# First attention of a two-layer kernel: row-paired score matmuls, and terms spread one batch earlier

## The reference, cut to what matters

```python
q = x @ Wq.T + bq ; k = x @ Wk.T + bk ; v = x @ Wv.T + bv     # 16 heads of 8
q = apply_rope(q) * scale ; k = apply_rope(k)
dots = einsum('bnih,bnjh->bnij', q, k)                        # 256 x 256 per head
dots = where(i < j, -100000.0, dots)                          # causal
attn = softmax(dots, axis=-1)
o = einsum('bnij,bnjh->bnih', attn, v)
out = o @ Wo.T + bo
```

## Time and profile before

| what | value |
|---|---|
| median of 3 runs | 1365.34 us (1360.61 to 1385.27) |
| the profiled execution | 1355.89 us |
| its span | 1354.0 us, 25150 instructions |
| first attention | from about 15 us to 444 us of the span |
| busy, TensorE / VectorE / ScalarE / POOL | 82% / 60% / 36% / 22% |
| mean granted TensorE clock | 0.88 of full speed |

### The profile page before, as it was taken

One profiled execution on the slowest core, in us unless ns is written; L12 is line 12 of the kernel. 1 busy time (PEld: TensorE's weight loads), 2 busy tenths in 40 slices (PEclk: granted clock), 3 DMA queues, 4 the chain that ended last, 5 costly groups with the idle time before them and its releaser, 6 DMA issues. The chain is left out here.

```text
span 1354.0 us, 25150 instructions
## 1 busy us (share of the span) xinstructions
PE 1105.7 (82%) x9345; PEld 654.5 (48%) x9345; DVE 815.0 (60%) x1910; ACT 483.5 (36%) x839; POOL 298.3 (22%) x283
## 2 busy tenths in 40 slices
PE   3699999999999599999999996588888889845140
PEld 2235454544444244444444442376777667744130
DVE  4456666646552466566666653488888888646322
ACT  0024444424445133323323321455555564411020
POOL 4132323213210000000000002342332321015536
PEclk9969999959999699999999998589999999855575
DMA  4534242422420622321332230323223322040233
GB/s 128 143 97 96 51 95 49 94 48 49 96 51 3 230 80 94 104 90 63 124 96 95 62 126 0 111 80 97 78 68 96 96 65 81 1 125 26 71 105 85
DMA packets 83989, 113.38 MB, mean 84 GB/s; under 512 B 9658, under 2 KB 53616, under 8 KB 81664
## 3 DMA queue, kind: packets, MB, share of 16 engines
q1 hardware_dynamic: 81840, 108.65, 28.5%
q0 software_dynamic: 2048, 3.37, 0.9%
HBM read 80.18 MB, written 32.65 MB: 83 GB/s over the span
## 5 line engine op out<-in xcount | busy, mean ns | idle before, releaser
L672 DVE TENSOR_REDUCE a_nmax<-ps 128x2 f32<-128x512 f32 (+1 forms) x192 | 132.4, 691 | 127.7 <-PE ps L513 88.2
L437 ACT ACTIVATE a_pr<-ps 128x512 f32<-128x512 f32 x192 | 114.2, 597 | 173.9 <-PE ps L488 124.9
L861 ACT ACTIVATE e_sg<-ps 128x512 f32<-128x512 f32 x136 | 81.2, 597 | 244.6 <-PE ps L886 231.5
L1050 DVE TENSOR_TENSOR e_up<-e_sg,ps 128x512 f32<-128x512 f32 x128 | 88.0, 687 | 106.9 <-PE ps L893 100.9
L886 PE MATMUL ps<-e_hT,e_wg 128*128 128x512 f32 x272 | 140.8, 600 | 0.8 <-DVE e_wT L1037 0.8
L902 PE MATMUL ps<-e_hm,e_wd 128*128 128x512 f32 x272 | 139.2, 594 | 1.4 <-DVE e_hm L1053 0.7
L472 PE MATMUL ps<-a_mask,identb 128*128 128x256 bf16 (+1 forms) x384 | 129.1, 336 | 13.5 <-DMA a_ks<-a_terms_d 9.4
L893 PE MATMUL ps<-e_hT,e_wu 128*128 128x512 f32 x272 | 139.8, 596 | 0.0
L1053 DVE TENSOR_TENSOR e_hm<-e_up,e_wb 128x512 f32<-128x512 f32 x128 | 88.5, 692 | 5.6
L902 PEld LDWEIGHTS ps<-e_hm,e_wd 128*128 128x128 f32 x272 | 51.5, 190 | 67.3 <-issue 63.5
L893 PEld LDWEIGHTS ps<-e_hT,e_wu 128*128 128x128 f32 x272 | 52.1, 191 | 65.6 <-issue 59.8
(11 more groups left out here) (266 smaller groups left out, 2031.6 us busy)
## 6 DMA issues: line engine op xcount, KB each, us to landing
e_wb<-e_wT_d SPq DMA_DIRECT2D x128, 256.0 KB, 3.3
a_gw<-a_gd_d SPq DMA_DIRECT2D x16, 1024.0 KB, 5.0
a_gd_d<-a_gc SPq DMA_DIRECT2D x64, 132.0 KB, 2.3
a_terms_d<-a_parts SPq DMA_DIRECT2D x32, 192.0 KB, 2.1
a_qs<-a_terms_d SPq DMA_DIRECT2D x16, 384.0 KB, 5.0
a_ks<-a_terms_d SPq DMA_DIRECT2D x16, 384.0 KB, 6.0
a_terms_d<-a_parts SPq DMA_DIRECT2D x32, 128.0 KB, 2.1
a_terms_d<-a_parts SPq DMA_DIRECT2D x32, 64.0 KB, 1.8
```

The costliest lines, as they stand in the source:

```text
L437: nc.scalar.activation(dst, src, ACT.Exp).then_inc(exp_done, 1)
L672: nc.vector.tensor_reduce(dst, src, AX_X, ALU.max, negate=True).then_inc(m_read, 1)
L861: nc.scalar.activation(sg[:, par], ps[:, 2 + par], ACT.Silu).then_inc(silu_done, 1)
L1050: nc.vector.tensor_tensor(up[:, par], sg[:, par], ps[:, 4 + par], ALU.mult).then_inc(up_done, 1)
```

## The change

In words:

1. **Pairs.** The terms of q and k are kept twice in `qs` and `ks`: in partitions 0 to 47 for C, and in partitions 64 to 111 (`M_ROW = 64`) for the maxima. The M score matmul gets `tile_position=(64, 0)`. TensorE's list now has 12 paired steps: both masks first, then the C and the M (or N) score matmuls alternating. C group 0 goes with M group 2, C 1 with M 3, C 2 with N 0, C 3 with N 1.
2. **Rows loaded in two goes.** `spread_parts` now loads the M rows alone. A new step `spread_again` loads the C rows of the same batch two bodies later; the store in DRAM, `terms_d`, has three buffers.
3. **A batch ahead.** Stage A is now b+4 and L is b+5; `last_part` moves from S to A, and `hT` has three buffers. The pipeline has one more body at its start. v's projection stays at b+2 and has its own semaphores.
4. **Order.** On POOL the list is now split_parts, last_part, rstd_of; before it was last_part, split_parts, rstd_of. On VectorE `rotate(0)` and `rotate(1)` move from before N(0,0) and N(0,1) to before and after N(1,0). On TensorE `project(0)` and `project(1)` move later in the body.
5. In the second attention and the second experts, some semaphores are merged into one; no instruction there changes.

The core of the diff:

```diff
+M_ROW = 64
-        hT = sb("hT", [P, L])
+        hT = sb("hT", [P, 3, L])
-        qs = sb("qs", [TOP + 3, 3, H, L], BF16)
+        qs = sb("qs", [M_ROW + ROWS, 3, H, L], BF16)
-        terms_d = nc.dram_tensor("a0_terms_d", [2, len(TERMS), P, L], BF16).ap()
+        terms_d = nc.dram_tensor("a0_terms_d", [3, 2, len(TERMS), P, L], BF16).ap()
...
-            ahead = {"D": -1, "C": 0, "M": 1, "N": 2, "S": 2, "A": 3, "L": 4}
+            ahead = {"D": -1, "C": 0, "M": 1, "N": 2, "S": 2, "A": 4, "L": 5}
...
-            pipeline(eng, -4, B + 1, 2, B - 4, body)
+            pipeline(eng, -5, B + 1, 2, B - 5, body)
...
+            def spread_again(b):
+                hold(sp, c_full, UN, b + -3, UN)
+                for dst, side in ((qs, 0), (ks, 1)):
+                    sp.dma_start(dst[0:ROWS, b.k % 3].rearrange("p h n -> p (h n)"), own_rows(side, b)
+                                 ).then_inc(c_spread, 16)
-            run(sp, [("S", spread_parts), ("M", spread_max)])
+            run(sp, [("S", spread_again), ("M", spread_max), ("A", spread_parts)])
...
             def last_part(b):
                 pool.wait_ge(summed, b.x * 4 + 4)
-                hold(pool, spread, SPREAD, b, 0)
-                hold(pool, c_full, UN, b + -2, 0)
+                hold(pool, m_spread, SPREAD, b, 0)
+                hold(pool, c_spread, SPREAD, b + -2, 0)
+                hold(pool, m_full, UN, b + -2, 0)
-            run(pool, [("S", last_part), ("A", split_parts), ("L", rstd_of)])
+            run(pool, [("A", split_parts), ("A", last_part), ("L", rstd_of)])
...
+            def scores(g, n, stage, gm):
+                ahead = {"M": 1, "N": 2}[stage]
+                def step(b):
+                    m = b + ahead
+                    has_c, has_m = 0 <= b.k < B, 0 <= m.k < B
+                    if has_c:
+                        open_c(g, n)(b)
+                    if has_m:
+                        open_m(gm, n)(m)
+                    for a in range(count_of(n)):
+                        if has_c:
+                            score_c(g, n, a, b)
+                        if has_m:
+                            score_m(gm, n, a, m)
                 return step
...
+            run(pe, [("B", scores(0, 0, "M", 2)), ("B", scores(0, 1, "M", 2)), ("B", scores(0, 2, "M", 2)),
+                     ("D", outputs(3)), ("S", project_values),
+                     ("B", scores(1, 0, "M", 3)), ("D", turn_outputs(0)), ("B", scores(1, 1, "M", 3)),
+                     ("A", turn_tokens), ("B", scores(1, 2, "M", 3)),
+                     ("C", outputs(0)), ("D", turn_outputs(1)),
+                     ("B", scores(2, 0, "N", 0)), ("D", turn_normal), ("B", scores(2, 1, "N", 0)), ("M", turn_max),
+                     ("B", scores(2, 2, "N", 0)), ("A", project(0)),
+                     ("C", outputs(1)), ("D", project_out),
+                     ("B", scores(3, 0, "N", 1)), ("A", project(1)), ("B", scores(3, 1, "N", 1)), ("D", turn_back),
+                     ("B", scores(3, 2, "N", 1)), ("C", outputs(2))])
...
-                    ("M", split_first), ("D", divide(1)), ("M", split_second), ("A", rotate(0)), ("M", split_third),
-                    ("N", maxima(0, 0)), ("M", split_last), ("A", rotate(1)),
-                    ("N", maxima(0, 1)), ("N", maxima(0, 2)), ("N", maxima(1, 0)),
-                    ("L", statistics), ("N", maxima(1, 1)), ("D", residual), ("N", maxima(1, 2)),
-                    ("L", normalise)])
+                    ("M", split_first), ("D", divide(1)), ("M", split_second), ("M", split_third), ("M", split_last),
+                    ("N", maxima(0, 0)), ("N", maxima(0, 1)), ("N", maxima(0, 2)), ("A", rotate(0)),
+                    ("N", maxima(1, 0)), ("A", rotate(1)), ("L", statistics), ("N", maxima(1, 1)), ("D", residual),
+                    ("N", maxima(1, 2)), ("L", normalise)])
```

More of the change, by code:

```diff
@@ L482, in step, with open_m @@
                     if n < 2:
[L484 to L489, removed]
[L490 to L497 removed]
+                        causal(bank.rearrange("p (j n) -> p j n", j=2)[:, :, 0:P], 1, 2)
+                    else:
+                        causal(bank.rearrange("p (j n) -> p j n", j=HJ), 1, HJ)
                 return step
[L500 removed]
+            def open_m(g, n):
                 def step(b):
[L502 removed]
                     if g == 0 and n == 0:
[L504 removed]
+                        pe.wait_ge(m_spread, b.x * SPREAD + SPREAD)
                     hold(pe, m_read, UN, b, 3 * g + n - 1)
@@ L522, in step, with count_of, score_c @@
-                    mm.then_inc(m_full, 1)
+                        causal(bank.rearrange("p (j n) -> p j n", j=2)[:, :, P:L], 0, 2)
+                    else:
+                        causal(bank.rearrange("p (j n) -> p j n", j=HJ), 0, HJ)
+                return step
+            def count_of(n):
+                return 2 if n < 2 else HJ
+            def score_c(g, n, a, b):
+                p, bank = b.k % 3, ps[:, 2 + (3 * g + n) % 2]
+                h = HG * ((2 * n if n < 2 else 0) + a) + g
+                out = bank.rearrange("p (a n) -> p a n", a=count_of(n))[:, a]
+                mm = nc.tensor.matmul(out, ks[0:TOP + 3, p, h, 0:P] if n < 2 else ks[0:TOP + 3, p, h, P:L],
+                                      qs[0:TOP + 3, p, h, :] if n < 2 else qs[0:TOP + 3, p, h, P:L],
+                                      start=False, stop=(a == count_of(n) - 1), skip_group_check=True)
+                if a == count_of(n) - 1:
+                    mm.then_inc(c_full, 1)
@@ new lines, in score_m @@
+            def score_m(g, n, a, b):
+                p, bank = b.k % 3, ps[:, (3 * g + n) % 2]
+                h = HG * ((2 * n if n < 2 else 0) + a) + g
+                out = bank.rearrange("p (a n) -> p a n", a=count_of(n))[:, a]
+                mm = nc.tensor.matmul(out, qs[M_ROW:M_ROW + ROWS, p, h, P:L] if n < 2 else qs[M_ROW:M_ROW + ROWS, p, h, 0:P],
+                                      ks[M_ROW:M_ROW + ROWS, p, h, :] if n < 2 else ks[M_ROW:M_ROW + ROWS, p, h, 0:P],
+                                      start=False, stop=(a == count_of(n) - 1), skip_group_check=True,
+                                      tile_position=(M_ROW, 0))
+                if a == count_of(n) - 1:
+                    mm.then_inc(m_full, 1)
@@ L563, in step, with project_values @@
                     pe.wait_ge(a_read, b.x * A_STEPS + which + 1)
[L564 to L573, removed]
+                    if which == 0:
+                        hold(pe, nT_read, 1, b, -2)
+                    for k in range(2):
+                        mm = nc.tensor.matmul(ps[:, 6, k * L:(k + 1) * L], w[:, 2 * which + k, :], hT[:, b.k % 3],
+                                              start=True, stop=True)
                     mm.then_inc(a_full, 1)
                 return step
+            def project_values(b):
+                if b.k + 1 < B:
+                    pe.wait_ge(a_read, b.x * A_STEPS + 2 * A_STEPS)
+                else:
+                    pe.wait_ge(nT_read, b.x - 1)
+                for k in range(TB):
+                    mm = nc.tensor.matmul(ps[:, 6, k * P:(k + 1) * P], hT[:, b.k % 3, k * P:(k + 1) * P], w[:, 4, :],
+                                          start=True, stop=True)
+                mm.then_inc(v_full, 1)
             def turn_outputs(k):
```

101 lines of the change are left out of this document (45 added, 56 removed).

## The result

The changed kernel takes 1370.83 us (median of 12 runs, 1364.25 to 1376.61) against 1361.72 us for the kernel before, timed beside it (12 runs, 1353.76 to 1385.27). The ratio is 1.0099, 95% interval [1.0069, 1.013]: slower by 1%, within the 2% band. The ratios in this document are taken from executions near the lowest time of their kernel alone, so they are not the quotients of the medians. The forecast was 1366.

The account below looks back on a forecast made before the run. A once-a-body loop through TensorE, VectorE and POOL was taken to bound the kernel at 22.4 us. From 1355.9: start +6, ten bodies -1, clock falls +24, end -18.5 gave 1366 us, range 1322 to 1412.

Parts of the forecast that it names:

- The main step: First attention: a loop through TensorE, rotate(1), POOL, normalise and one maxima sets the body at 22.4 us, against 22.46 before.
- the first rival: The gain comes through: POOL is done before VectorE asks, bodies of about 18.2 us, total 1300; chance 0.12.
- The pairs: TensorE's paired scores overlap in array halves: 0.65 us instead of 1.07, four-block 0.87 instead of 1.30, saving 5.1 a body.
- The rival of no overlap: The array halves do not overlap: pairs cost 0.21 us more each, total 1392; chance 0.05.
- The clock: After each TensorE gap of 5 us, 6.8 us at 1.2 GHz: 2.4 us a body, bounds 0 and 11.4.
- the bound of 11.4 a gap: Upper bound of the clock's cost per body: 27.3 us at 1.2 GHz, as after the 3.4 us gap.
- The clock stays down: Slower rival: the third pair's gap sets off long falls; 1389 us if half the ten bodies, 1435 if all; chance 0.20.
- The sum, against the profiled execution's 1355.9: Start +6, ten bodies with the loop -1, ten falls of the clock +24, end -18.5: +10.5, giving 1366 us.
- The other parts: spread_again ... 0: Two added loads of 0.39 MB a body, queued on SP ahead of spread_max, were said to cost 0.
- the last three near 15.5: Batches 13 to 15 have no A and L ahead, the loop is open: 46.5 us instead of 65.0, -18.5.
- one of the prediction's own signs of being wrong: TensorE waiting for DMA loads at the first pair would show the forecast wrong.
- The start: The added body has no scores; stage L of the second batches waits for one longer POOL chain: +6, bounds 0 and +12.

Follow-up runs that it names:

- run 4: Changed kernel with 20 idle matmuls before the third pair's second mask in bodies 1 to 11: 1352.27 us, ratio 1.0012 to the kernel before.
- run 6: Changed kernel with normalise moved behind the next body's maxima(3,0) on VectorE and spread_max ahead of spread_again on SP: 1285.78 us, ratio 0.9456.
- run 2: Changed kernel with normalise moved on VectorE from the body's end to behind maxima(3,0) of the next body: 1330.55 us, ratio 0.9872.
- run 3: Changed kernel with C scores directly behind the C mask and M scores directly behind the M mask, so nothing is paired: 1432.07 us, ratio 1.0615.
- run 8: Changed kernel with normalise behind the next body's maxima(3,0), spread_max ahead of spread_again, and scores not paired: 1351.69 us, ratio 0.9951.
- run 7: Changed kernel with normalise behind the next body's maxima(3,0), spread_max ahead of spread_again, and POOL's rstd_of ahead of last_part: 1288.24 us, ratio 0.9471.

## Why the prediction was right, and where it was not

**The main step held.** The chain from the third pair's mask over project(1), the second rotation, POOL and normalise back to the mask was given 22.4 us; run 4 shows it at 22.8, without falls of the clock. Its pieces: TensorE from the mask to the second rotation 13.0 forecast, 13.25 in run 4 (229.73 to 242.98); POOL 7.1 forecast, 7.3 measured; normalise 0.60, both; the gap "about 5 us before the third pair's mask", 5.12; VectorE's wait before normalise, released by POOL's rstd, 4.85. What it means was shown by taking the loop away (run 6: 18.4 us, where the first rival had given 18.2 for that case).

**The pairs.** 0.65 us forecast, 0.63 measured; with four blocks 0.87 and 0.88 (237.91 to 238.79 in run 4). The saving of 5.1 us of TensorE's work a body is 17.2 busy in run 2 against 21.9, 4.7. The rival of no overlap is out by the starting times, and by runs 3 and 8.

**The clock.** Forecast 2.4 us a body, measured 24.9 - 22.8 = 2.1. The stretches are 6.8 and 10.2 us, and the falls of 27.3 us, which carried the slower rival, did not come. In the ten bodies the work done at 1.2 GHz is 3.4 to 6.6 us, 4.9 on average (6.42, 4.60 and 3.72 in the windows above), so 2.1 is 0.44 a microsecond, near the 0.42 of the forecast. The penalty of half of the throttled time, which the Trainium skill's "TensorE: Matmul & The Clock Gate" states in its section "HAM oscillation — how this bites in real kernels", would give 2.4 for these 4.9 us, and more if the idle part of each fall is counted in; the trace is below it.

**A row read too far.** The 27.3 us at 1.2 GHz from 65.4 on the earlier trace rows are no fall from work at 2.4 GHz behind a gap of 3.4 us. The stretch at 1.00 ahead of them is the gap itself, without work, and TensorE was slow before it. A mask of 256 columns took 57.80 - 57.47 = 0.33 us there, against 0.21 at 260.02; the trace has the granted clock only from 62.0 on.

```profile
57.47 0.40 PE L472 MATMUL ps<-a_mask,identb 128*128 128x256 bf16 x1
57.80 0.60 PE L513 MATMUL ps<-a_ks,a_qs 48*128 48x256 bf16 x2
```

So the bound of 11.4 a gap and the rival "The clock stays down" had one row for them and not two, the fall at 277.0, and that one follows no gap. That no long fall came in the changed kernel does not exclude it: in run 3 a gap of 3.12 us (to 159.90) was followed by 23.9 us at 1.2 GHz.

**Two terms of the sum were wrong, and offset each other.**

- "The sum, against the profiled execution's 1355.9": ten bodies were priced at 22.4 + 2.4 against 22.5. But in the profile used these ten contain the fall at 277, so they took 236.2 us, 23.6 each. The term should have been +11.8, not +23. Measured against that profile: +13.1. The text priced that fall at 11.4 and did not take it out of the baseline.
- "The other parts: spread_again ... 0" and "the last three near 15.5". Two of the three are 17.0 and 14.5, as forecast for an open loop, but one is 24.9: with no gap at the third pair to hide in, the maxima's parts landed late behind both loads, TensorE waited 7.76 us, and the clock fell for 10.2. Measured -8.5 for the three, not -18.5. A wait of TensorE for this DMA at the first pair was one of the prediction's own signs of being wrong, and it came here and at 88.12. The text named the queue and its cover and still set the cost at nothing for the very bodies in which the cover goes.

The start, +6 forecast, is +6.6, but that is luck in part: the forecast was for one longer POOL chain, and 2.4 of the 6.6 are a body with the gap and the fall. The 6.1 us in the later stages were not forecast. No instruction there changed. With the changed kernel's code these stages last 910.7 us (run 6) to 919.4 (run 7), a scatter that covers the 6.1; the kernel before has one profile, 909.7, so a small cost of the merged semaphores is not excluded.

So the forecast was right for its reason, and closer than it deserved: it had some 11 us too much in the ten bodies and 10 too little in the last three.

## What to carry to other kernels

Before pairing or speeding up the busiest engine, follow what each in-order engine has queued behind its waits: here 5 us of TensorE's work were saved, and moves of the steps that fed it gave more than all of it back through the least busy engine. A wait belongs where nothing urgent stands behind it; moving one step on VectorE and one on SP turned +1% into -5.4%. And an idle gap on TensorE has to be priced twice, once as time and once as clock, and a small DMA issued behind large ones had to wait for them here.

## What the runs showed of the hardware that was not expected

- 24 KB stored behind four loads of 384 KB took 8.5 us from its issue to the next step, against 2.8 with no load issued for 8 us before it (run 2). In the changed kernel it was 9.1 us (391.76 to 400.83), in a kernel whose bodies have a mean DMA share of 0.5.
- The 51-row scores in partitions 0 to 50 and the 48-row scores in partitions 64 to 111 start within 0.01 us of each other; the second kind costs nothing measurable. The scores of a pair take 227.06 - 226.74 = 0.32 us, and two C scores without a partner in the last bodies also 429.48 - 429.16 = 0.32.
- Idle stretches of TensorE and what followed, where it had run at 2.4 GHz: 0.8 to 1.3 us (runs 4 and 6) and 2.13 (run 7, at 178.2) kept 2.4 GHz, though the earlier trace rows has 2.1 followed by 6.8 us at 1.2 GHz; 2.51 was followed by 6.8 (run 6) or 3.4 (run 7); 3.5 (run 3) by 6.8; about 5 (the changed kernel) by 6.8 or 10.2. But 3.12 (run 3, at 156.8) was followed by 23.9, and the 27.3 us at 277.0 came after no gap, so the length of a gap does not tell the length of the fall.
- At the start TensorE runs at the slow pace (a mask of 256 columns 0.33 instead of 0.21 us) until some 93 us before, 98 in the changed kernel, and 148 and 143 with the pairs taken apart (runs 3 and 8). No run here shows what ends it.
- normalise takes 0.60 us with POOL idle, and its first half alone 1.17 beside a POOL instruction: shortening a wait by 1.6 us gave only about 1.
